# Windowed attention on one core: six buffers, a new slot table, and tokens ordered in column pairs

## The chip, the cores and the metric

The kernel runs on one NeuronCore of one Trainium2 chip. The core has five engines that work at the same time, each on its own queue of instructions: TensorE (PE in the rows, with PEld for its weight loads), VectorE (DVE), ScalarE (ACT), GpSimd (POOL) and SyncE (SP), which here issues all DMAs. They wait for each other on semaphores. The metric is the device time of one execution in microseconds (us), lower is better.

## The reference

Two layers of the same kind act on 64 images of 14 x 14 tokens with 192 channels. Each adds to x an attention of 12 heads of 16 channels over a group norm of x, with a bias of relative positions that is worked out from the query:

```python
x = x + _L0_conv_ref(_gn(x), ...)
x = x + _L1_conv_ref(_gn(x), ...)

qkv = x.reshape(b, hw, dim) @ qkv_w + qkv_b
rel_h = jnp.einsum('bhwc,hkc->bhwk', r_q, Rh)
rel_w = jnp.einsum('bhwc,wkc->bhwk', r_q, Rw)
attn_bias = (rel_h[:, :, :, :, None] + rel_w[:, :, :, None, :]).reshape(b * nH, hw, hw)
attn = jnp.einsum('bqd,bkd->bqk', q, k) * scale + attn_bias
attn = jax.nn.softmax(attn, axis=-1)
out = jnp.einsum('bqk,bkd->bqd', attn, v)
return out @ proj_w + proj_b
```

`rel_h` depends on the image row of the query, so its products take the queries of one image row (14 tokens that lie side by side); `rel_w` depends on the image column (14 tokens that lie 14 apart).

## The kernel before, in words

A unit is one image in one layer, 128 in all. The program is written out as a software pipeline: iteration i has twelve slots, and a job that stands at slot number `at` for its unit is issued in slot `at % 12` of an iteration that is `at // 12` later (negative: earlier) than the unit's own. So jobs of some seven units stand side by side in one iteration, and what an engine does in a slot is fixed by the tables: `JOBS`, `PV_AT`, `MAX_AT`, `EXP_AT` for TensorE, `ACT_LATER` and `DVE_LATER` for the readers of TensorE's results, `POOL_AT` and `SP_AT`. An engine never passes over an instruction that waits: what stands behind it waits too.

TensorE in every slot does one head of the score product for the maxima (`ps_max`, L525) and one head of the score product for the exponentials (`ps_sc`, L538), and then the jobs of that slot:

- xT: transposes the input `xa` (L429), ScalarE copies it to `xT`, VectorE takes statistics (L743), GpSimd the channel's moments (L809, L812);
- g: sums them over a channel group (L435), VectorE copies the result (`gsm`, L791), GpSimd works out the norm (L819 to L830), `xn` (L838), and its float16 halves `xn_hi`, `xn_lo` (L846, L851);
- qk0, qk1, v: projections (L412); queries and keys go as two float16 halves (`qk_hl`, L598 and L734) through DRAM into `q_st` and `k_st`;
- rel0, rel1, rel2: products of q with the position tables for 6, 6 and 2 image rows and as many image columns (L471). Per row or column two row products and two column products, one for each half of the heads, into four groups of 32 PSUM partitions. ScalarE cuts them into a high half (L634 the rows, L643 the columns), VectorE subtracts for the low half (`rel_hl`, L776), and SP brings them into `q_st`;
- mT0, mT1: transposes of the maxima of six heads (L480), ScalarE scales them to `mrow` (L610), and SP brings them into `q_st` as a row of the score product (m0, m1). `ps_sc` of head 0 waits for m0, of head 6 for m1;
- PV: probabilities times v (`ps_o`, L557), ot: transposes of the result (L491), VectorE divides (`rsum` L755, `on` L759), oT: transposes back (L501), y: output projection (L412), ScalarE `yr` (L657), GpSimd adds x to it (`yo`, L862).

The jobs share three PSUM banks. The third entry of a job in `JOBS` is its bank, and `bank_free` makes TensorE wait until the job that had this bank last has been read; the fourth entry says by which semaphore. `ps_max` has two buffers, so the maxima product of a head waits for VectorE's maximum (L722) two heads back.

Input is loaded twice, as `xa` for the transposes and as `xd` for the addition at the end. `q_st`, `k_st` and `v_st` have four buffers each.

## Time and profile before

| | |
|---|---|
| median of 3 runs | 2341.02 us (2326.52 to 2341.86) |
| the profiled execution | 2339.97 us, its span 2338.2 us |
| TensorE busy | 2094.7 us (90%) |
| VectorE busy | 1653.4 us (71%) |
| ScalarE busy | 1621.4 us (69%) |
| GpSimd busy | 714.4 us (31%) |
| DMA moved | 216.34 MB |

The span reaches from the first to the last instruction. Busy time is a share of that span; matmuls overlap, so TensorE's own share says that its queue is seldom empty, not that it works at its peak. In the timelines below a row is one instruction or a run of like ones ("x24"), with its start, the time from the start of the first to the end of the last, and, in brackets, how long the engine was idle before it and what ended that.

### The profile page before, as it was taken

To read this page: it belongs to the slowest core of one execution; us is meant where nothing else is said; L and a number is where in the kernel's file an instruction comes from. 1 tells how busy PE (TensorE), PEld (TensorE's weight loads), DVE (VectorE), ACT (ScalarE), POOL (GpSimd) and SP (SyncE) were. 2 spreads that over 40 slices of the span, in tenths; PEclk is the share of its full clock that TensorE was granted. 3 is DMA by queue.
4 is the path that set the end of the run, shared out by engine and by line. 5 is a ranking of instruction groups with operands and counts; after the bars stand their busy time and mean duration, and the time that the engine had idled before them with its cause. 6 is when DMAs were issued, how large, how long until landed. Compare 5 with 4: busy or idle time off the path is not lost.

```text
span 2338.2 us, 73485 instructions
## 1 busy us (share of the span) xinstructions
PE 2094.7 (90%) x27904; PEld 1595.9 (68%) x27904; DVE 1653.4 (71%) x3923; ACT 1621.4 (69%) x3713; POOL 714.4 (31%) x1796
## 2 busy tenths in 40 slices
...
GB/s 47 84 94 95 104 91 105 91 92 91 103 93 97 90 94 93 101 93 93 91 98 91 94 103 96 88 96 100 91 91 102 94 100 93 94 93 103 91 92 47
DMA packets 170550, 216.34 MB, mean 93 GB/s; under 512 B 29783, under 2 KB 138072, under 8 KB 170202
## 3 DMA queue, kind: packets, MB, share of 16 engines
...
q14 instruction: 122, 1.00, 0.2%
...
## 4 chain that ended last, share of the span: by engine, by line
PE 39%; DMA 33%; SPq 14%; DVE 6%; issue 4%; ACT 3%; POOL 1%; POOLq 0%; ACTq 0%; DVEq 0%
PE ps_m L412 18%; DMA q_st<-mrow 17%; DMA k_dram<-qk_hl 10%; PE ps_sc L538 7%; PE ps_max L525 6%; SPq L375 6%; DMA q_dram<-qk_hl 6%; DVE qk_hl L734 4%; PE ps_o L557 3%; SPq L382 3%; ACT qk_hl L598 2%; SPq L341 2%; SPq L387 2%; PE ps_m L501 2%; DVE rel_hl L776 1%
## 5 line engine op out<-in xcount | busy, mean ns | idle before, releaser
L722 DVE TENSOR_REDUCE mx<-ps_max 98x2 f32<-98x392 f32 x1536 | 819.4, 562 | 232.6 <-PE ps_max L525 215.5
L586 ACT ACTIVATE probs<-ps_sc 98x392 f32<-98x392 f32 x1536 | 714.5, 497 | 232.3 <-PE ps_sc L538 198.2
L525 PE MATMUL ps_max<-k_st,q_st 124*98 124x196 f16 x3072 | 548.9, 261 | 82.4 <-DVE mx L722 82.1
L538 PE MATMUL ps_sc<-q_st,k_st 125*98 125x196 f16 x3072 | 523.3, 252 | 95.6 <-DMA q_st<-mrow 94.1
L776 DVE TENSOR_TENSOR rel_hl<-ps_m,rel_hi 64x504 f16<-64x504 f32 (+1 forms) x768 | 431.4, 562 | 162.0 <-ACT rel_hi L643 152.9
L525 PEld LDWEIGHTS ps_max<-k_st,q_st 124*98 124x98 f16 x3072 | 295.0, 126 | 296.4 <-issue 198.0
L538 PEld LDWEIGHTS ps_sc<-q_st,k_st 125*98 125x98 f16 x3072 | 320.9, 126 | 123.1 <-DMA q_st<-mrow 120.4
L557 PE MATMUL ps_o<-probs,v_st 98*32 98x196 f32 x6144 | 389.6, 340 | 0.5 <-ACT o_sb L578 0.5
L634 ACT ACTIVATE rel_hi<-ps_m,is_lo 64x504 f16<-64x504 f32 (+1 forms) x384 | 223.9, 583 | 189.1 <-PE ps_m L471 185.7
L471 PE MATMUL ps_m<-q_st,rel_st 64*32 64x84 f16 x7168 | 341.6, 266 | 4.8 <-DVE rel_hl L776 4.5
L809 POOL TENSOR_TENSOR msq<-mv 96x2 f32<-96x2 f32 x128 | 24.4, 191 | 1007.1 <-DVE mv L748 1007.1
L643 ACT ACTIVATE rel_hi<-ps_m,is_lo 64x504 f16<-64x504 f32 (+1 forms) x384 | 226.0, 589 | 4.7
L471 PEld LDWEIGHTS ps_m<-q_st,rel_st 64*32 64x32 f16 x7168 | 174.9, 99 | 76.4 <-DVE rel_hl L776 5.1
L557 PEld LDWEIGHTS ps_o<-probs,v_st 98*32 98x32 f32 x6144 | 134.4, 108 | 135.6 <-issue 74.9
L734 DVE TENSOR_TENSOR qk_hl<-ps_m,qk_hl 128x392 f16<-128x392 f32 (+1 forms) x256 | 107.1, 459 | 149.3 <-ACT qk_hl L598 149.3
L412 PE MATMUL ps_m<-xn_hi,w_hi 98*128 98x196 f16 (+1 forms) x768 | 193.5, 252 | 10.5 <-POOL xn_lo L851 10.5
L412 PE MATMUL ps_m<-xn_lo,w_hi 96*128 96x196 f16 x768 | 192.3, 250 | 0.0
L412 PE MATMUL ps_m<-xn_hi,w_lo 96*128 96x196 f16 x768 | 191.7, 250 | 0.0
L819 POOL TENSOR_TENSOR msq<-gsm 96x2 f32<-96x2 f32 x128 | 24.6, 192 | 481.7 <-DVE gsm L791 481.7
L598 ACT CAST qk_hl<-ps_m 128x392 f16<-128x392 f32 (+1 forms) x256 | 103.6, 405 | 86.5 <-PE ps_m L412 83.3
L491 PE MATMUL ps_m<-ident,o_sb 128*98 128x68 f32 x1536 | 151.7, 247 | 0.4 <-ACT o_sb L578 0.4
L862 POOL TENSOR_TENSOR yo<-yr,xd 98x384 f32<-98x384 f32 x128 | 128.0, 1000 | 60.5 <-ACT yr L657 60.5
...
## 6 DMA issues: line engine op xcount, KB each, us to landing
q_st<-q_dram SPq DMA_DIRECT2D x128, 294.0 KB, 3.8
...
q_dram<-qk_hl SPq DMA_DIRECT2D x128, 147.0 KB, 2.6
k_dram<-qk_hl SPq DMA_DIRECT2D x128, 147.0 KB, 2.7
...
```

Of the source, the lines that this page charges most:

```text
L412: last = nc.tensor.matmul(dst, weights(a, c, k), moving(b, c, k), start=n == 0, stop=n == len(terms) - 1)
L471: last = nc.tensor.matmul(to, rel_st[:, lay, axis, w:w + RW], q[:, :, a * SIDE:a * SIDE + SIDE] if axis == 0 else q[:, :, a::SIDE], start= ...
L491: last = nc.tensor.matmul(ps[0:HT, at:at + HG * (HD + 1)], o_sb[p2][:, g, h * HT:h * HT + HT], ident[:, :].rearrange("p (j x) -> p j x", x ...
L525: last = nc.tensor.matmul(ps_max[head % 2][0:HT, h * TOK:h * TOK + TOK], q_st[u.r][0:R_MAX, head, h, :], k_st[u.r][0:R_MAX, head, :], star ...
L538: last = nc.tensor.matmul(ps_sc[head % 2][0:HT, kt * TOK:kt * TOK + TOK], k_st[u.r][0:STACK, head, kt * HT:kt * HT + HT], q_st[u.r][0:STAC ...
L557: last = nc.tensor.matmul(ps_o[32 * j:32 * j + 32, 0:TOK], v_st[u.r][:, kt, head_of(head), :], p[:, kt, :], start=kt == 0, stop=kt == 1)
L586: nc.scalar.activation(probs[head][:, :, :], ps_sc[head % 2][0:HT, 0:2 * TOK].rearrange("p (k t) -> p k t", k=2), ACT.Exp, scale=1.0 / (QS ...
L634: nc.scalar.activation(dst, src, ACT.Identity, scale=is_lo[0:64, 0:1])
L643: nc.scalar.activation(dst, src, ACT.Identity, scale=is_lo[64:128, 0:1])\
L722: nc.vector.reduce_max(mx[u.r % 2][:, head, :], ps_max[head % 2][0:HT, 0:2 * TOK].rearrange("p (q k) -> p q k", q=2), axis=AX.X).then_inc( ...
L734: nc.vector.tensor_tensor(qk_hl[u.r % 2][:, 1, at, :], ps_m[BANK[f"qk{j}"]][:, 0:len(tiles) * TOK].rearrange("p (c t) -> p c t", t=TOK), q ...
L776: last = nc.vector.tensor_tensor(l, src, h, ALU.subtract)
```

## The change

1. **Token order.** Within each pair of image rows the tokens now stand column by column: token (2k + r, b) is at place 28k + 2b + r instead of 14(2k + r) + b. ScalarE puts them so when it copies `xT` out of PSUM, and back when it copies `o_sb`. A column product now reads runs of two elements, 28 apart, where it read single ones, 14 apart; a row product reads every second element where it read 14 side by side. The same holds for where they write in PSUM (for rel0 and rel1; rel2's row products write 84 in a row).
2. **Buffers.** `q_st`, `k_st`, `v_st` have six buffers, `xa` has eight; `xd` and its DMA are gone, and GpSimd adds `xa`.
3. **Slots and banks.** All slot tables and the order of the jobs change; so do the three banks.
4. **Setup.** The one-hot rows of `k_st` are copied from a float16 tile in the new order, 72 copies instead of 48, and two more `v_st` are set.

```diff
+VB = 6
+QB = 6
+XB = 8
...
-        LEAD, TAIL = 1, 6
-        MAX_AT, EXP_AT = 28, 40
...
+        LEAD, TAIL = 2, 7
+        MAX_AT, EXP_AT = 30, 42
+
+        PV_AT = {(0, 0): 45, (0, 1): 46, (1, 0): 50, (1, 1): 52, (2, 0): 55, (2, 1): 55}
+        O_LATER = 2
+
+        JOBS = [(36, "mT0", 0, (s_mrow, 2, 1)),
+                (1, "qk0", 2, (s_qklo, 2, 1)),
...
-        ACT_LATER = {"qk": 0, "mT": 1, "oT": 0, "xT": 0, "rel": 0, "v": 0, "y": 0}
-        DVE_LATER = {"bn": 2, "g": 0, "ot": 0, "oT": 0, "qk": 0, "rel": 0}
-
-        POOL_AT = {"mv": -11, "group": -3, "xn": -1, "xhi": 0, "xlo": 0, "y": 63}
+        ACT_LATER = {"qk": 0, "mT": 0, "oT": 0, "xT": 0, "rel": 0, "v": 0, "y": 1}
+        DVE_LATER = {"bn": 3, "g": 0, "ot": 0, "oT": 3, "qk": 1, "rel": 1}
+
+        POOL_AT = {"mv": -6, "group": -3, "xn": -1, "xhi": 2, "xlo": 5, "y": 82}
         QK_TILES = ((0, 1), (2,))

-        SP_AT = {"m0": 39, "m1": 46, "rel": 22, "qk_out": 3, "q_in": 3, "k_in": 4, "xd": 55, "out": 69, "xa": -12}
+        SP_AT = {"m0": 39, "m1": 41, "rel": 23, "qk_out": 6, "q_in": 7, "k_in": 6, "out": 80, "xa": -15}
...
                                 if axis == 0:
-                                    to = to.rearrange("p (h a b) -> p h a b", h=HH, a=rows)[:, :, i, :]
+                                    to = to.rearrange("p (h k b r) -> p h k r b", h=HH, r=2, b=SIDE)[:, :, i // 2, i % 2, :]
+                                    q = q.rearrange("p h (k b r) -> p h k r b", r=2, b=SIDE)[:, :, a // 2, a % 2, :]
                                 else:
-                                    to = to.rearrange("p (x b) -> p x b", b=rows)[:, :, i]
...
+                                    to = to.rearrange("p (x b r) -> p x b r", b=rows, r=2)[:, :, i, :]
+                                    q = q.rearrange("p h (k b r) -> p (h k) b r", r=2, b=SIDE)[:, :, a, :]
+                                last = nc.tensor.matmul(to, rel_st[:, lay, axis, w:w + RW], q, start=True, stop=True)
...
-            for i in range(UNROLL):
+            dve.wait_ge(s_oh, 1)
+            for i in range(QB):
                 for head in range(HEADS):
-                    nc.vector.tensor_copy(k_st[i][R_REL:STACK, head, :], oh_raw[R_REL:STACK, :])
+                    nc.vector.tensor_copy(k_st[i][R_REL:STACK, head, :], oh_f16[R_REL:STACK, :])
...
-                        nc.gpsimd.tensor_tensor(yo[p2][:, :, :], yr[p2][:, :, :], xd[p2][:, :, :], ALU.add)\
+                        nc.gpsimd.tensor_tensor(yo[p2][:, :, :], yr[p2][:, :, :], xa[u.n % XB][:, :, :], ALU.add)\
```

The slots of an iteration, in which TensorE's jobs stand (numbers modulo twelve; every slot begins with one head of `ps_max` and one of `ps_sc`, and PV stands last in its slot):

| slot | before | of the change |
|---|---|---|
| 0 | y | mT0 |
| 1 | PV | qk0 |
| 2 | | qk1, PV |
| 3 | qk0, qk1, xT, PV | y, xT |
| 4 | | PV |
| 5 | rel0, mT1 | |
| 6 | rel1, PV twice | rel0, mT1 |
| 7 | g | rel1, PV twice |
| 8 | ot, rel2, PV | g |
| 9 | PV | ot, rel2, PV |
| 10 | oT, v | oT, PV |
| 11 | mT0 | v |

The job g of the next unit and ot of an earlier one, as they stand in TensorE's queue behind rel1 and its PV, before. The rows give line, operation, output and inputs, shape, and the semaphores that are waited for; `s_mrow` tells that ScalarE has read the maxima's transposes, `s_rlo` that VectorE has read a rel result:

```order
L557 MATMUL ps_o<-probs,v_st 32x196 x7
L525 MATMUL ps_max<-k_st,q_st 98x196 [waits s_mx]
L525 MATMUL ps_max<-k_st,q_st 98x196
L538 MATMUL ps_sc<-q_st,k_st 98x196 [waits s_p]
L538 MATMUL ps_sc<-q_st,k_st 98x196
L435 MATMUL ps_m<-mv,gmat 96x4 [waits s_mrow,s_mv]
L525 MATMUL ps_max<-k_st,q_st 98x196 [waits s_mx]
L525 MATMUL ps_max<-k_st,q_st 98x196
L538 MATMUL ps_sc<-q_st,k_st 98x196 [waits s_p]
L538 MATMUL ps_sc<-q_st,k_st 98x196
L491 MATMUL ps_m<-ident,o_sb 98x68 [waits s_rlo,s_o]
```

The same place of the change (L433 is g, L488 is ot; `s_g` tells that VectorE has read g's result):

```order
L554 MATMUL ps_o<-probs,v_st 32x196 x7
L522 MATMUL ps_max<-k_st,q_st 98x196 [waits s_mx]
L522 MATMUL ps_max<-k_st,q_st 98x196
L535 MATMUL ps_sc<-q_st,k_st 98x196 [waits s_p]
L535 MATMUL ps_sc<-q_st,k_st 98x196
L433 MATMUL ps_m<-mv,gmat 96x4 [waits s_rlo,s_mv]
L522 MATMUL ps_max<-k_st,q_st 98x196 [waits s_mx]
L522 MATMUL ps_max<-k_st,q_st 98x196
L535 MATMUL ps_sc<-q_st,k_st 98x196 [waits s_p]
L535 MATMUL ps_sc<-q_st,k_st 98x196
L488 MATMUL ps_m<-ident,o_sb 98x68 [waits s_g,s_o]
```

The order of the jobs is the same, but g is now in the bank of rel0 and waits for its reader, and ot is in the bank of g and waits for g's reader; before, g had the bank of mT1 and ot that of rel0.

VectorE's queue at the same place, before (L776 is `rel_hl`, in turn of rel0 and rel1, L791 reads g):

```order
L776 TENSOR_TENSOR rel_hl<-ps_m,rel_hi 64x6x84 [waits s_rhi,s_rel0]
L776 TENSOR_TENSOR rel_hl<-ps_m,rel_hi 64x84x6
L722 TENSOR_REDUCE mx<-ps_max 98x2 [waits s_sm_ps]
L776 TENSOR_TENSOR rel_hl<-ps_m,rel_hi 64x6x84 [waits s_rhi]
L776 TENSOR_TENSOR rel_hl<-ps_m,rel_hi 64x84x6
L722 TENSOR_REDUCE mx<-ps_max 98x2 [waits s_sm_ps]
L791 COPY gsm<-ps_m 96x4 [waits s_gp,s_g_ps]
L722 TENSOR_REDUCE mx<-ps_max 98x2 [waits s_sm_ps]
L755 RECIPROCAL rsum<-ps_m 98x24 [waits s_ot_ps]
```

And of the change:

```order
L725 TENSOR_REDUCE mx<-ps_max 98x2 [waits s_sm_ps]
L779 TENSOR_TENSOR rel_hl<-ps_m,rel_hi 64x6x84 [waits s_rhi,s_rel3]
L779 TENSOR_TENSOR rel_hl<-ps_m,rel_hi 64x42x12
L725 TENSOR_REDUCE mx<-ps_max 98x2 [waits s_sm_ps]
L779 TENSOR_TENSOR rel_hl<-ps_m,rel_hi 64x6x84 [waits s_rhi]
L779 TENSOR_TENSOR rel_hl<-ps_m,rel_hi 64x42x12
L794 COPY gsm<-ps_m 96x4 [waits s_gp,s_g_ps]
L725 TENSOR_REDUCE mx<-ps_max 98x2 [waits s_sm_ps]
L758 RECIPROCAL rsum<-ps_m 98x24 [waits s_ot_ps]
```

The copy of g's result stands directly behind the second subtraction of rel1, where a maximum stood between them; the subtraction of rel0 stands one slot later, behind one more maximum.

GpSimd's queue of the change, over one unit (L864 is the addition that ends a unit, `yo`). Before, `yo` stood ahead of the first L819, behind the moments:

```order
L822 TENSOR_TENSOR msq<-gsm 96x2 [waits s_g]
L825 TENSOR_TENSOR gvar<-gsm,msq 96x2 [waits s_gp]
L828 TENSOR_TENSOR gvar<-gvar,eps 96x2 [waits s_gp]
L831 TENSOR_TENSOR rstd<-gvar,halfpow 96x2 [waits s_gp]
L833 TENSOR_SCALAR nmean<-gsm 96x2
L864 TENSOR_TENSOR yo<-yr,xa 98x384 [waits s_out1,s_yr]
L839 TENSOR_TENSOR anchor<-eps 96x2 [waits s_gp]
L841 TENSOR_SCALAR xn<-xT,nmean,rstd 96x196 x2
L848 TENSOR_TENSOR anchor<-eps 96x2 [waits s_v_ps,s_xn]
L849 CAST xn_hi<-xn 96x392
L854 TENSOR_TENSOR xn_lo<-xn,xn_hi 96x392 [waits s_xhi]
```

The addition has moved between the work on g's result and `xn`, so it stands ahead of what qk0 waits for.

## Rows read from the trace of the kernel before

**Rows 1.** The page's shares: busy us, share of span, instructions.

```profile
PE 2094.7 (90%) x27904; PEld 1595.9 (68%) x27904; DVE 1653.4 (71%) x3923; ACT 1621.4 (69%) x3713; POOL 714.4 (31%) x1796
```

**Rows 2.** One line's view, ot: count, ns min/median/max, first and last start.

```profile
L491 PE MATMUL ps_m<-ident,o_sb x1536: 223/248/302, 115.0 to 2328.5; 128*98 128x68 f32 x192
```

**Rows 3.** Waits: who waited for whom, total us, times, longest.

```profile
PE ps_sc L538 <- DMA q_st<-mrow: 94.1, 105, 2.1
```

**Rows 4.** Timeline of TensorE over one unit: start, length, instruction.

```profile
1005.63 1.10 PE L471 MATMUL ps_m<-q_st,rel_st 64*32 64x84 f16 x24
1006.66 0.25 PE L480 MATMUL ps_m<-ident,mx 98*12 98x98 f32 x1
...
1009.38 0.26 PE L435 MATMUL ps_m<-mv,gmat 96*96 96x4 f32 x2
1010.27 0.37 PE L525 MATMUL ps_max<-k_st,q_st 124*98 124x196 f16 x2 [0.63 <-DVE mx L722]
...
1010.65 1.18 PE L491 MATMUL ps_m<-ident,o_sb 128*98 128x68 f32 x12
1011.76 0.47 PE L471 MATMUL ps_m<-q_st,rel_st 64*32 64x84 f16 x8
1012.17 0.54 PE L557 MATMUL ps_o<-probs,v_st 98*32 98x196 f32 x8
...
1014.55 0.37 PE L538 MATMUL ps_sc<-q_st,k_st 125*98 125x196 f16 x2 [0.60 <-DMA q_st<-mrow]
...
1016.09 0.33 PE L525 MATMUL ps_max<-k_st,q_st 124*98 124x196 f16 x2
...
1022.80 1.10 PE L471 MATMUL ps_m<-q_st,rel_st 64*32 64x84 f16 x24
```

**Rows 5.** Timeline of ScalarE at the same place.

```profile
1006.77 0.68 ACT L634 ACTIVATE rel_hi<-ps_m,is_lo 64x504 f16<-64x504 f32 x1 [0.49 <-PE ps_m L471]
...
1008.56 0.23 ACT L610 ACTIVATE mrow<-ps_m 12x98 f16<-12x98 f32 x1
...
1016.29 0.48 ACT L649 COPY v_st<-ps_m 98x384 f32<-98x384 f32 x1 [0.47 <-PE ps_m L412]
```

**Rows 6.** Timeline of VectorE at the same place.

```profile
1008.24 1.38 DVE L776 TENSOR_TENSOR rel_hl<-ps_m,rel_hi 64x504 f16<-64x504 f32 x2 [1.17 <-ACT rel_hi L643]
1009.65 0.57 DVE L722 TENSOR_REDUCE mx<-ps_max 98x2 f32<-98x392 f32 x1
1010.25 1.37 DVE L776 TENSOR_TENSOR rel_hl<-ps_m,rel_hi 64x504 f16<-64x504 f32 x2
...
1012.14 0.15 DVE L791 COPY gsm<-ps_m 96x4 f32<-96x4 f32 x1
...
1012.68 0.29 DVE L755 RECIPROCAL rsum<-ps_m 98x24 f32<-98x24 f32 x1
1013.01 0.62 DVE L759 TENSOR_TENSOR on<-ps_m,rsum 98x192 f32<-98x192 f32 x2
```

**Rows 7.** Timeline of GpSimd at the same place.

```profile
1007.57 1.00 POOL L862 TENSOR_TENSOR yo<-yr,xd 98x384 f32<-98x384 f32 x1
1012.37 0.19 POOL L819 TENSOR_TENSOR msq<-gsm 96x2 f32<-96x2 f32 x1 [3.79 <-DVE gsm L791]
...
1016.16 0.93 POOL L851 TENSOR_TENSOR xn_lo<-xn,xn_hi 96x392 f16<-96x392 f32 x1
```

**Rows 8.** Windows, L471 alone: stretch, length, PE busy (instructions it touches), PEld, clock.

```profile
1005.63:1005.85 0.22, 0.22 (x16) 0.22 (x18) 1.00 0.00 0
```

**Rows 9.** Timeline of TensorE at the start, at the half clock: rel0 with rel1.

```profile
60.59 2.02 PE L471 MATMUL ps_m<-q_st,rel_st 64*32 64x84 f16 x48 [0.25 <-DVE qk_hl L734]
```

**Rows 10.** TensorE's timeline, one unit later: the wait for m1.

```profile
1032.38 0.50 PE L538 MATMUL ps_sc<-q_st,k_st 125*98 125x196 f16 x2 [1.25 <-DMA q_st<-mrow]
```

**Rows 11.** Windows: PE, PEld, DVE, ACT, POOL busy (instructions), granted clock.

```profile
1032.50:1035.90 3.40, 3.40 (x22) 3.38 (x22) 0.64 (x2) 1.38 (x3) 1.59 (x4) 0.50 0.42 95
1015.30:1018.70 3.40, 3.40 (x45) 3.00 (x43) 2.01 (x4) 2.49 (x8) 1.63 (x4) 1.00 0.41 96
```

More of the change, by code:

```diff
@@ L107, in attention_kernel @@
         anchor = sb("anchor", [CC, 3])
-        q_st = [sb(f"q_st{i}", [128, HEADS, 2, HT], F16) for i in range(4)]
-        k_st = [sb(f"k_st{i}", [128, HEADS, TOK], F16) for i in range(4)]
-        v_st = [sb(f"v_st{i}", [HT, 2, HEADS, PW]) for i in range(4)]
+        q_st = [sb(f"q_st{i}", [128, HEADS, 2, HT], F16) for i in range(QB)]
+        k_st = [sb(f"k_st{i}", [128, HEADS, TOK], F16) for i in range(QB)]
+        v_st = [sb(f"v_st{i}", [HT, 2, HEADS, PW]) for i in range(VB)]
         def pair(name, shape, dt=F32):
             return [sb(f"{name}{i}", shape, dt) for i in range(2)]
-        xa = pair("xa", [HT, 2, C])
+        xa = [sb(f"xa{i}", [HT, 2, C]) for i in range(XB)]
         xT = pair("xT", [CC, 2, TOK])
@@ L143, in attention_kernel @@
         oT_lo = pair("oT_lo", [CC, 2, TOK], F16)
-        xd = pair("xd", [HT, 2, C])
         yr = pair("yr", [HT, 2, C])
@@ L161, in attention_kernel @@
         s_wlo = sem("s_wlo")
+        s_oh = sem("s_oh")
         s_setup = sem("s_setup")
@@ L239, in run @@
                 iteration(lambda lag, i=i: Unit(0, i - lag), min(max(i, 0) // SAMPLES, LAYERS - 1))
-        LEAD, TAIL = 1, 6
-        MAX_AT, EXP_AT = 28, 40
-        PV_AT = {(0, 0): 44, (0, 1): 45, (1, 0): 49, (1, 1): 51, (2, 0): 54, (2, 1): 54}
-        O_LATER = 1
-        JOBS = [(60, "y", 0, (s_yr, 1, 1)),
-                (3, "qk0", 1, (s_qklo, 2, 1)),
-                (3, "qk1", 0, (s_qklo, 2, 2)),
-                (-9, "xT", 2, (s_xT, 1, 1)),
-                (17, "rel0", 0, (s_rlo, 3, 1)),
-                (41, "mT1", 2, (s_mrow, 2, 2)),
-                (18, "rel1", 1, (s_rlo, 3, 2)),
-                (-5, "g", 2, (s_g, 1, 1)),
-                (56, "ot", 0, (s_on, 1, 1)),
-                (20, "rel2", 1, (s_rlo, 3, 3)),
-                (58, "oT", 2, (s_olo, 1, 1)),
-                (10, "v", 0, (s_v, 1, 1)),
-                (35, "mT0", 1, (s_mrow, 2, 1))]
+        LEAD, TAIL = 2, 7
[4 more added lines that the diff above has]
+                (1, "qk0", 2, (s_qklo, 2, 1)),
+                (2, "qk1", 0, (s_qklo, 2, 2)),
+                (63, "y", 2, (s_yr, 1, 1)),
+                (-9, "xT", 1, (s_xT, 1, 1)),
+                (18, "rel0", 0, (s_rlo, 3, 1)),
+                (42, "mT1", 1, (s_mrow, 2, 2)),
+                (19, "rel1", 2, (s_rlo, 3, 2)),
+                (-4, "g", 0, (s_g, 1, 1)),
+                (57, "ot", 0, (s_on, 1, 1)),
+                (21, "rel2", 2, (s_rlo, 3, 3)),
+                (58, "oT", 1, (s_olo, 1, 1)),
+                (11, "v", 0, (s_v, 1, 1))]
         ORDER = [name for _, name, _, _ in JOBS]
@@ L357, in iteration @@
                                 p, r0 = 64 * axis + 32 * half, R_REL + RW * axis
-                                sp.dma_start(q_st[u.r][r0:r0 + rows, half * HH:half * HH + HH, :, :],
+                                sp.dma_start(q_st[u.n % QB][r0:r0 + rows, half * HH:half * HH + HH, :, :],
                                              rel_hl[u.r % 2][p:p + rows, :, :]).then_inc(s_rel[u.r], 16)
@@ L374, in iteration @@
                         for part in range(2):
-                            sp.dma_start(k_st[u.r][2 * HD * part:2 * HD * part + 2 * HD, :, :],
+                            sp.dma_start(k_st[u.n % QB][2 * HD * part:2 * HD * part + 2 * HD, :, :],
                                          k_dram[u.r].rearrange("l d h c t -> d l (h c t)"))\
                               .then_inc(s_kst[u.r], 16)
-                    u = due(unit, s, SP_AT["xd"])
-                    if u:
-                        src, at = (x_in, u.n) if not layer_of(u, layer) else (x1, u.n - SAMPLES)
-                        wait(sp, s_y, u.n - 1)
-                        sp.dma_start(xd[u.r % 2][:, :, :], tokens(src[bass.ds(at, 1)])).then_inc(s_xd[u.r], 16)
                     u = due(unit, s, SP_AT["out"])
@@ L462, in job @@
                             for half in range(2):
-                                q = q_st[u.r][0:R_REL, half * HH:half * HH + HH, :, :]\
+                                q = q_st[u.n % QB][0:R_REL, half * HH:half * HH + HH, :, :]\
                                     .rearrange("p h q t -> p h (q t)")
@@ L647, in iteration @@
                         act.wait_ge(s_v_ps, u.n + 1)
-                        wait(act, s_o_ps, (u.n - 3) * GROUPS)
-                        nc.scalar.copy(v_st[u.r][:, :, :, 0:HD],
+                        wait(act, s_o_ps, (u.n - VB + 1) * GROUPS)
+                        nc.scalar.copy(v_st[u.n % VB][:, :, :, 0:HD],
                                        ps_m[BANK["v"]][0:HT, 0:2 * C]
```

44 lines of the change are left out of this document (22 added, 22 removed).

## The prediction

> **What bounds the kernel now.** I read four views in this order. The page's shares say that TensorE is busy 90% of the span; VectorE's 1653.4 us are 12.9 us for each of 128 units, ScalarE's 1621.4 us are 12.7 [rows 1]. The first and the last start of job ot, which runs once in each unit, give the pace: (2328.5 - 115.0) / 127 = 17.43 us per unit [rows 2]. What lies outside is 2338.2 - 2213.5 = 124.7 us. TensorE's timeline shows one unit from rel0 at 1005.63 to the next at 1022.80, 17.17 us [rows 4]. In it TensorE waits twice: from the end of g (9.38 + 0.10) to 10.27, which is 0.79 us, for VectorE's maximum, and before `ps_sc` of head 6 for the DMA of the maxima m1 (the row's 0.60 us, 0.77 us by starts, since two pipelined products hide some). The second wait varies: 94.1 us over 105 times, up to 2.1 [rows 3]. Without either a unit is 17.17 - 0.79 - 0.77 = 15.61 us of TensorE's own work. So TensorE's queue is the bound, with two waits in it, and the timelines of the others [rows 5 to 7] show why the first is there: rel0 starts on TensorE at 5.63, ScalarE at 6.77, VectorE at 8.24, and VectorE has two subtractions of 1.4 us to do with maxima between them.
>
> **Part 1, the column products.** rel0 has 24 products and lasts from 1005.63 to 1006.66, rel2 has 8 and lasts from 1011.76 to 1012.17 [rows 4]: 0.62 us for 16 more, 0.155 us per image row with its column, and 1.03 - 6 x 0.155 = 0.10 around them. In the first 0.22 us 16 of the 24 products have begun [rows 8]; the remaining 8 take 0.8. The row products run ahead in their own PSUM partitions, and the column products set the pace at 0.155 per pair. At the half clock 48 products take 2.02 us where 24 take 1.10 at the full clock [rows 9, 4], no longer per product, so it is access to memory and not the array that costs. With runs of two there are half as many places to go to. Bounds: 0.155 (nothing gained) and 0.04 (8 row products in 0.22 us are 0.03 per product; a pair at most this); I take the half, 0.077, since the price followed the places. Then rel0 and rel1 take 6 x 0.077 + 0.10 = 0.56, rel2 0.25: TensorE's work falls by 0.47 + 0.47 + 0.16 = 1.10 us, to 14.5 us per unit.
>
> The Trainium skill, "SBUF — State Buffer", section Specifications (TRN2), says that SBUF has lines of 16 bytes and wants at least two hits on each for full bandwidth; by it runs of two float16 go at the full rate, rel0 takes 0.34 instead of 0.56, and the sum below falls by about 0.3 us a unit. The rows cannot decide between that and the half.
>
> **Part 2, buffers.** `xd` goes with one DMA a unit, and the extra buffers remove no wait that the rows show. m1 is issued right after its maxima, six slots before its reader, where it was issued in the reader's slot behind k_in, xd and out. Its wait of 0.77 us goes. SP's queue gets a wait for a landing (k_in right behind qk_out) and one for `yo`, with q_in, out, xa, rel and m0 behind them; their readers stand five slots and more later, except m0's, which is in the sixth slot after it. I cost all this at nothing, since those slots cover it; if m0 were late, it would cost what m1 costs now, up to 0.77.
>
> **Part 3, the slots.** What matters is the chain from rel0 to ot. Count from rel0's first product. Before: ScalarE +1.14, VectorE +2.61 to +3.99, second subtraction +4.62 to +5.99, g's copy +6.51 to +6.66, ot at +5.02 [rows 4, 5, 6]; ot did not have to wait for g's copy, it had the bank of rel0. In the change:
> - rel0 ends at +0.56, the transpose mT1 behind it +0.29 later (0.25 and 0.04 to hand over) at +0.85. ScalarE now scales mT1 first (0.23, done +1.10), then does the two halves of rel0 at 0.68 each, to +2.48; VectorE starts at +2.58 and ends at +3.96. So the faster rel0 buys nothing here: the mT1 in front of it takes its place.
> - TensorE's g waits for that: +4.00, where its queue is ready at 0.56 + 0.09 + 0.43 + 0.56 + 0.81 (two PV) + 0.38 = +2.83. A wait of 1.17.
> - VectorE: maximum, 0.60 as now from 9.65 to 10.25, second subtraction +4.57 to +5.95, g's copy to +6.12. TensorE's ot waits for it: **+6.17**. Ready at 4.09 + 0.38 = +4.47: a wait of 1.70.
> - From ot to the next rel0 stands the same work as before, in another order: 1010.65 to 1022.80 is 12.15, less 0.77 of m1 and 0.16 of rel2: 11.22. Three small waits are new in it. oT (one slot behind ot, was two): ot takes 1.11, VectorE starts 0.17 later and needs 0.95 (12.68 to 13.63), so oT can start 2.28 after ot; TensorE is there after ot, rel2, a PV of 0.47 and a head pair of 0.38, 2.21: 0.07. mT0 now has v's bank: ScalarE's copy of v starts 0.20 after v's end (1016.09 to 1016.29), takes 0.48, 0.05 to hand over, and one head pair of 0.34 covers part: 0.39. qk0 needs `xn_lo`: GpSimd takes 12.37 to 17.09 from g's copy, 4.72 us [rows 7], and `yo` is moved into this stretch, 1.00 more, so qk0 can start at 6.12 + 0.08 + 5.72 + 0.05 = +11.97; by the like pieces of the timeline TensorE is there at +11.9: 0.07.
>
> **Sum: 6.17 + 11.22 + 0.53 = 17.92 us per unit**, of which TensorE waits 3.4, against 1.56 in the unit shown (14.5 + 3.4 agrees). The costs end in ot's wait: what is late next is GpSimd's `xn_lo`, and with it qk0.
>
> **Part 4, the clock.** After the two waits of this unit TensorE's granted clock stayed full; where it had waited 1.25 us for m1 one unit later [rows 10], the clock stood at 0.50, 1.2 GHz instead of 2.4, in the 3.40 us that followed, with 22 instructions against 45 in an equal stretch at full clock [rows 11]. That is 1.7 us lost. In the change TensorE waits 1.17 and then 1.70 us in every unit with 0.5 us of work between. I expect the lower level behind it in most units: 8 in 10, at 1.5 us each (part of a stretch may lie in the wait), is +1.2, less 0.1 of small waits it covers. **Per unit 19.0 us.**
>
> **Part 5, setup.** 24 more copies of 196 columns: at most a maximum's 0.57 us each [rows 6], 14 us, at least nothing if the float16 source makes all 72 faster. The source is half as wide; I take 5.
>
> **Total.** 1.8 us around the span, 124.7 + 5 outside the pace, 127 x 19.0 = 2413: **2545 us**, 205 above the profiled execution of 2339.97, which lies 1 us below the median 2341.02.
>
> **Rivals.**
> - *The same chain, full clock.* 131.5 + 127 x 17.92 = 2407. For it: before, waits of 0.8 did not lower the clock. Against: 1.25 did.
> - *The chain is shorter.* If VectorE or ScalarE get through sooner, so that ot starts near +5.7, and the small waits stay, a unit is 17.4 and the time 2341: no change.
> - *Row products pay.* They now read and write every second element. Should each place in PSUM cost as a column product does now, the row pair goes at 0.155, rel0 stays 1.03: chain +0.47, rel2 +0.16, so +0.6 a unit, 2621. The Trainium skill, "PSUM — Partial Sum Buffer", section Specifications (TRN2), says that lines are 8 bytes and that any access that is not contiguous slows matmuls significantly, which is this; no row shows such an access alone.
> - *Faster, the other side.* If my chain is wrong in its main link and ot does not wait behind VectorE (its wait under about 0.9 decides, at full clock, since then gains of 1.10 + 0.77 win), a unit comes to 15.3, with VectorE's 12.9 below it: 131.5 + 1943 = 2075. Against it stand the queue order and the durations of [rows 6], none of which the change shortens.
>
> **Chances.** Chain with low clock 0.47, chain at full clock 0.22, row products 0.11, shorter chain 0.07, faster 0.13. The range takes the first three: 2395 to 2640. Above 1% is what a measurement of this kernel tells from no change. Faster by over 1%: 0.13. Within 1%: 0.06. Slower: 0.81.
>
> **What would show it.** Right: TensorE's largest waits are g for `rel_hl` (about 1 us a unit) and ot for `gsm` (about 1.5), both absent now; the waits for m1 are gone; rel0's 24 products take 0.56; the mean granted clock falls from 0.98 to about 0.9, in stretches right behind ot's start. GpSimd's `xn_lo` appears as what ends a wait of qk0. Wrong: TensorE's ot starts less than 5.6 us behind rel0, or the wait for `gsm` is under 0.5 us a unit; then the pace is TensorE's own work, near 15. Rows at 0.155 a pair would show as rel0 at 1.0 us.

## The result and the profile after

| | before | after |
|---|---|---|
| median | 2337.26 us (4 runs, 2326.52 to 2341.86) | 2832.02 us (4 runs, 2829.27 to 2835.07) |
| ratio | | 1.2125, 95% interval 1.2076 to 1.2174 |
| span of the profiled execution | 2338.2 us | 2827.7 us |
| mean granted clock of TensorE | 0.98 | 0.798 |
| one unit, from starts of ot | 17.43 us | 21.25 us |

The change makes the kernel 21% slower. The direction was forecast; the size was not: 2545 us, with 2640 as the upper end. Executions more than 1.5% above the fastest of their kernel count as slow, and ratios and medians here go by the others.

The shares on the page of after, and the granted clock in 40 slices of the span:

```profile
PE 2418.8 (86%) x27904; PEld 1856.1 (66%) x27904; DVE 1688.4 (60%) x3950; ACT 1609.7 (57%) x3713; POOL 708.7 (25%) x1796
...
PEclk9777877877887787788778778877877887787788
```

TensorE is busy for longer than before [rows 1] with the same number of instructions, though its column products are cheaper. The digits of the clock say why: 7 and 8 all through.

The line of ot, in the view of one line, and the waits of TensorE by line, in us, times and the longest:

```profile
L488 PE MATMUL ps_m<-ident,o_sb x1536: 248/273/434, 119.0 to 2817.9; 128*98 128x68 f32 x192
```

```profile
PE ps_m L488 <- DVE gsm L794: 185.9, 123, 1.5
PE ps_m L433 <- DVE rel_hl L779: 142.7, 126, 2.1
...
PE ps_m L477 <- ACT v_st L649: 5.5, 25, 0.3
```

The pace is (2817.9 - 119.0) / 127 = 21.25 us, 3.82 above [rows 2]; 127 times that is 485 of the 489.5 us between the spans. The first two rows are the two waits that were forecast, one of each in nearly every unit, and the waits for m1 [rows 3] have no row any more.

TensorE's timeline over one unit of after (L471 rel, L477 mT, L433 g, L488 ot, L554 PV):

```profile
1014.29 0.62 PE L471 MATMUL ps_m<-q_st,rel_st 64*32 64x84 f16 x24
1014.85 0.25 PE L477 MATMUL ps_m<-ident,mx 98*12 98x98 f32 x1
...
1018.39 0.30 PE L433 MATMUL ps_m<-mv,gmat 96*96 96x4 f32 x2 [1.12 <-DVE rel_hl L779]
...
1020.58 2.23 PE L488 MATMUL ps_m<-ident,o_sb 128*98 128x68 f32 x12 [1.51 <-DVE gsm L794]
1022.75 0.46 PE L471 MATMUL ps_m<-q_st,rel_st 64*32 64x84 f16 x8
1023.14 0.88 PE L554 MATMUL ps_o<-probs,v_st 98*32 98x196 f32 x8
...
1029.70 0.24 PE L477 MATMUL ps_m<-ident,mx 98*12 98x98 f32 x1
...
1036.00 0.63 PE L471 MATMUL ps_m<-q_st,rel_st 64*32 64x84 f16 x24
```

The same stretch in windows (stretch, length, busy time of PE, PEld, DVE, ACT, POOL with instructions, then the granted clock, the share that the DMA engines are busy, and GB/s):

```profile
1014.00:1018.00 4.00, 3.27 (x78) 2.13 (x75) 3.27 (x10) 3.88 (x9) 0.38 (x2) 1.00 0.13 27
1018.00:1022.00 4.00, 2.10 (x15) 1.96 (x16) 2.80 (x6) 1.78 (x4) 1.25 (x4) 0.68 0.49 119
1022.00:1026.00 4.00, 4.00 (x37) 2.37 (x36) 2.06 (x6) 1.76 (x4) 3.84 (x9) 0.50 0.53 130
1026.00:1030.00 4.00, 3.99 (x28) 3.47 (x25) 1.13 (x2) 1.43 (x5) 0.06 (x1) 0.54 0.39 101
1030.00:1034.00 4.00, 4.00 (x51) 3.53 (x49) 3.01 (x6) 2.49 (x7) 0.00 (x0) 1.00 0.00 1
```

The clock falls from 2.4 to 1.2 GHz within the stretch that holds the second wait (in halves of a microsecond it is 0.94 in 1019.0:1019.5 and 0.50 from then on, so here it falls some 0.4 us into that wait), and stays there through ot, rel2, the probability products, oT and all of v. ot's twelve products take 2.17 us to the start of rel2, where they took 1.11 before [rows 4]. It is full again by 1030, some 9 us behind ot's start. That is the rule and not this unit alone: the mean clock of 0.798 means 2 x 0.202 x 2827.7 = 1142 us at half speed, and the trace has 126 stretches at the lower level, 9.1 us long on average, one for nearly each of the 128 units. The kernel before has 20, of 5.1 us on average.

ScalarE and VectorE behind rel0 in after:

```profile
1015.13 0.24 ACT L609 ACTIVATE mrow<-ps_m 12x98 f16<-12x98 f32 x1
1015.40 0.68 ACT L634 ACTIVATE rel_hi<-ps_m,is_lo 64x504 f16<-64x504 f32 x1
```

```profile
1016.87 1.37 DVE L779 TENSOR_TENSOR rel_hl<-ps_m,rel_hi 64x504 f16<-64x504 f32 x2 [0.68 <-ACT rel_hi L643]
1018.27 0.57 DVE L725 TENSOR_REDUCE mx<-ps_max 98x2 f32<-98x392 f32 x1
1018.87 1.37 DVE L779 TENSOR_TENSOR rel_hl<-ps_m,rel_hi 64x504 f16<-64x504 f32 x2
1020.28 0.16 DVE L794 COPY gsm<-ps_m 96x4 f32<-96x4 f32 x1
```

Counted from rel0's start at 1014.29, ScalarE's first half stands at +1.11, the subtractions at +2.58 and +4.58, g at +4.10, ot at +6.29.

### The profile page after: what moved, and what is told of

Read it like the earlier page. It is cut to its first block, busy times and chain, and to the rows that moved or that the text cites. A ratio compares the mean times of both kernels' runs of the same rounds, so it can differ in the third digit from the quotient of the medians.

```text
span 2827.7 us, 73380 instructions
## 1 busy us (share of the span) xinstructions
PE 2418.8 (86%) x27904; PEld 1856.1 (66%) x27904; DVE 1688.4 (60%) x3950; ACT 1609.7 (57%) x3713; POOL 708.7 (25%) x1796
## 4 chain that ended last, share of the span: by engine, by line
PE 64%; DVE 16%; ACT 11%; issue 7%; POOL 1%; ACTq 0%; DMA 0%; DVEq 0%; SPq 0%; POOLq 0%
PE ps_m L410 21%; DVE rel_hl L779 12%; PE ps_o L554 11%; PE ps_max L522 10%; PE ps_m L488 8%; PE ps_sc L535 8%; ACT rel_hi L643 3%; ACT rel_hi L634 3%; PE ps_m L498 3%; DVE mx L725 2%; ACT probs L585 2%; PE ps_m L427 2%; ACT o_sb L575 1%; PE ps_m L471 1%; PE ps_m L477 1%
## 5 line engine op out<-in xcount | busy, mean ns | idle before, releaser
L522 PE MATMUL ps_max<-k_st,q_st 124*98 124x196 f16 x3072 | 619.7, 289 | 0.4 <-DVE mx L725 0.4
L535 PE MATMUL ps_sc<-q_st,k_st 125*98 125x196 f16 x3072 | 589.1, 278 | 0.7 <-ACT probs L585 0.7
L554 PE MATMUL ps_o<-probs,v_st 98*32 98x196 f32 x6144 | 475.1, 403 | 1.7 <-ACT o_sb L575 0.9
L535 PEld LDWEIGHTS ps_sc<-q_st,k_st 125*98 125x98 f16 x3072 | 385.5, 146 | 3.5 <-ACT probs L585 2.6
L488 PE MATMUL ps_m<-ident,o_sb 128*98 128x68 f32 x1536 | 218.0, 309 | 191.0 <-DVE gsm L794 185.9
L488 PEld LDWEIGHTS ps_m<-ident,o_sb 128*98 128x98 f32 x1536 | 197.8, 219 | 213.9 <-issue 207.4
L554 PEld LDWEIGHTS ps_o<-probs,v_st 98*32 98x32 f32 x6144 | 145.5, 119 | 132.5 <-issue 87.1
L471 PE MATMUL ps_m<-q_st,rel_st 64*32 64x84 f16 x7168 | 221.3, 266 | 2.9 <-DVE rel_hl L779 2.7
L410 PE MATMUL ps_m<-w_hi,xn_hi 98*98 98x192 f16 (+1 forms) x512 | 187.6, 366 | 0.3 <-DVE gsm L794 0.3
L410 PE MATMUL ps_m<-w_lo,xn_hi 96*98 96x192 f16 x512 | 187.6, 366 | 0.0
L410 PE MATMUL ps_m<-w_hi,xn_lo 96*98 96x192 f16 x512 | 187.6, 366 | 0.0
```

The costliest lines, as they stand in the source:

```text
L410: last = nc.tensor.matmul(dst, weights(a, c, k), moving(b, c, k), start=n == 0, stop=n == len(terms) - 1)
L471: last = nc.tensor.matmul(to, rel_st[:, lay, axis, w:w + RW], q, start=True, stop=True)
L488: last = nc.tensor.matmul(ps[0:HT, at:at + HG * (HD + 1)], o_sb[p2][:, g, h * HT:h * HT + HT], ident[:, :].rearrange("p (j x) -> p j x", x ...
L522: last = nc.tensor.matmul(ps_max[head % 2][0:HT, h * TOK:h * TOK + TOK], q_st[u.n % QB][0:R_MAX, head, h, :], k_st[u.n % QB][0:R_MAX, head ...
L535: last = nc.tensor.matmul(ps_sc[head % 2][0:HT, kt * TOK:kt * TOK + TOK], k_st[u.n % QB][0:STACK, head, kt * HT:kt * HT + HT], q_st[u.n % ...
L554: last = nc.tensor.matmul(ps_o[32 * j:32 * j + 32, 0:TOK], v_st[u.n % VB][:, kt, head_of(head), :], p[:, kt, :], start=kt == 0, stop=kt == 1)
```

## The experiments

**1. How much is chain, how much is clock.** My theory was that the chain of waits gives the pace at full clock and the rest is the clock. So I left every wait's end where it is and gave TensorE something to do until then: unread score products, into the buffer that its next maxima product overwrites.

```diff
+            def filler(unit, s, n):     # n products of the next head, read by nobody
+                ...
+                    for i in range(n):
+                        nc.tensor.matmul(ps_max[head % 2][0:HT, i % 2 * TOK:i % 2 * TOK + TOK], ...)
...
                     for name in ORDER:
+                        if due(unit, s, AT[name]) and name in ("g", "ot"):
+                            filler(unit, s, {"g": 12, "ot": 16}[name])
                         job(name, unit, s, layer)
```

> The changed kernel with products that nobody reads in its two waits: 12 ahead of g and 16 ahead of ot, copies of the next head's maxima product into the free ps_max buffer, about 1.0 and 1.35 us at full clock, less than the waits of 1.1 and 1.5 us that they stand in. The chain of waits is not touched. Theory (the waits lengthen the unit to about 18 us, and the rest, 3.3 us a unit, is TensorE's clock, which is low behind them): the mean granted clock goes back to 0.97 or more, a unit takes 17.9 to 18.2, the time is 2400 to 2450 us. Rival (the 3.3 us come from something else, contention or more waits further on): the clock does not matter, and the time stays at 2800 or more.

Measured: 2395.38 us (ratio to before 1.0225, 1.0172 to 1.0278), clock 0.998, with 3516 more matmuls than after. Its timeline and its line of ot:

```profile
1011.48 0.63 PE L471 MATMUL ps_m<-q_st,rel_st 64*32 64x84 f16 x24
...
1014.30 1.17 PE L517 MATMUL ps_max<-k_st,q_st 124*98 124x196 f16 x12
...
1016.10 1.53 PE L517 MATMUL ps_max<-k_st,q_st 124*98 124x196 f16 x16
1017.77 0.45 PE L488 MATMUL ps_m<-ident,o_sb 128*98 128x68 f32 x3
```

```profile
L488 PE MATMUL ps_m<-ident,o_sb x1536: 225/248/312, 117.1 to 2384.1; 128*98 128x68 f32 x192
```

ot starts at +6.29, as in after, yet the unit is (2384.1 - 117.1) / 127 = 17.85 us against 21.25. So of after's 3.82 us, 0.42 is the chain and 3.40 is the clock: 53 and 432 us of the whole. (The 17.43 of before holds a clock loss of its own: at a mean clock of 0.978 it spends 0.8 us of a unit at half speed, worth 0.4 at most. With full clock on both sides the chain costs up to 0.8.) Work that nobody reads makes the kernel 437 us faster than waiting.

**2. Which wait, and what stands behind it.** Two kernels: the filler ahead of ot alone, and no filler in the waits but twelve unread products behind ot, ahead of rel2.

```diff
+                        if due(unit, s, AT[name]) and name in {"ot": 16}:       # e9_filler_ot
+                        if due(unit, s, AT[name]) and name in {"rel2": 12}:     # e9b_filler_behind
```

> The changed kernel with the unread products ahead of ot alone (16, about 1.35 us); the wait of 1.1 us ahead of g stays empty. With both filled the clock was 0.998 and a unit 17.85 us. Theory A (either wait alone is like those of the kernel before, which lowered the clock now and then): clock 0.93 to 0.99, 18.0 to 18.7 us a unit, 2415 to 2510 us. Theory B (one wait of 1.1 us in each unit is enough to keep the clock low): 2650 or more.

> The changed kernel with 12 unread maxima products (1.0 us at full clock, 2.0 at half) not in a wait but behind ot, ahead of rel2, where TensorE has work. Both long waits stay. If only the waits decide how long the clock stays low, a unit is 1 to 2 us longer than 21.25: 2950 to 3080 us. If the work that stands behind the waits (transposes, products with 32 weights) is what lets the clock stay low for 6.8 to 10.2 us, the added work pays for itself: at or below 2830.

Measured: 2423.17 us for the first (1.0365, 1.0284 to 1.0446), clock 0.975, with g's wait untouched:

```profile
PE ps_m L433 <- DVE rel_hl L791: 142.3, 126, 2.5
```

A wait of 1.12 us in each unit alone leaves the clock nearly full (23 stretches at the lower level in the whole trace, against 126). With the second one, of 1.51, which begins 0.7 us behind the first, it falls in nearly every unit. No run keeps the second wait and fills the first, so whether 1.51 us would do it alone is not shown; the single waits of 1.6 and 1.7 us of experiment 3 do. The second kernel (one execution): 2723.4 us, clock 0.907. TensorE around ot:

```profile
1005.43 1.67 PE L488 MATMUL ps_m<-ident,o_sb 128*98 128x68 f32 x12 [1.51 <-DVE gsm L806]
1006.89 2.17 PE L517 MATMUL ps_max<-k_st,q_st 124*98 124x196 f16 x12
1008.99 0.46 PE L471 MATMUL ps_m<-q_st,rel_st 64*32 64x84 f16 x8
1009.38 0.55 PE L566 MATMUL ps_o<-probs,v_st 98*32 98x196 f32 x8
```

```profile
1009.00:1009.50 0.50, 0.50 (x13) 0.24 (x16) 0.00 (x0) 0.00 (x0) 0.42 (x3) 0.54 0.79 228
```

Both waits are there (184.1 and 143.7 us in all), and the clock still falls (in this unit 0.6 us behind ot's start: 0.55 in 1006.0:1006.5), but PV at 1009.38 takes 0.55 where after's takes 0.88: the level is full again 4 us behind ot's start instead of 9. Over the whole trace there are 126 stretches at the lower level as in after, but of 4.0 us on average instead of 9.1. Per unit it costs (2712.0 - 116.4) / 127 = 20.44, less 17.85, less some 1.0 for the twelve added products: 1.6 instead of 3.4. So adding work behind the wait takes 109 us off, and with the waits unchanged, other work behind them changed how long the clock stays low. The one instance in before did not tell this. There, behind the wait of 1.25 us [rows 10], stood this:

```profile
1032.68 0.86 PE L501 MATMUL ps_m<-ident,on 98*96 98x98 f32 x4
1033.33 0.36 PE L412 MATMUL ps_m<-w_hi,xn_hi 98*98 98x192 f16 x1
...
1035.90 0.25 PE L480 MATMUL ps_m<-ident,mx 98*12 98x98 f32 x1
```

v's twelve products came at once, and mT0 behind them is at full speed. In after 6.3 us of ot, rel2, PV and oT come first, and again it is behind v that the clock is full. (That wait was also another one, 1.25 us alone, so these two instances differ in more than the work behind.) Which property of ot, rel2 and PV keeps it low was not told apart.

**3. One number of the table.** If g's place in the banks makes ot late, moving g back should undo it in after and do it in before.

```diff
-                (-4, "g", 0, (s_g, 1, 1)),      # after: e2_g_bank1
+                (-4, "g", 1, (s_g, 1, 1)),
-                (-5, "g", 2, (s_g, 1, 1)),      # before: e3_before_g_bank0
+                (-5, "g", 0, (s_g, 1, 1)),
```

> The changed kernel with g in bank 1 (where the transposes of the maxima stand) instead of bank 0: g no longer waits for rel0's reader, and ot waits for rel0's reader instead of g's. Theory (the banks of g and ot make the two long waits, and these lower the clock): the waits of g for rel_hl and of ot for gsm go; ot starts about 4.0 us behind rel0 instead of 6.3, but rel2 then waits for rel1's reader, oT for on, qk0 for xn_lo, each under 1 us, so a unit takes 17.2 to 18.0 at a clock above 0.95: 2320 to 2450 us. Rival (the slot table as a whole is at fault, whatever the bank): 2750 or more.

> The kernel before with one number changed: g in bank 0, so that g waits for rel0's reader and ot for g's. Theory: ot starts 6.6 to 6.7 us behind rel0 instead of 5.0, with a wait of about 1.6 us for gsm that was not there, and the clock falls behind it as in the changed kernel: 19 us a unit from the wait and 2 to 3 more from the clock, 2700 to 2900 us. Rival (buffers, token order or GpSimd's order make the loss): within 2% of before, 2300 to 2390.

Measured on before: 2820.47 us (1.2039, 1.1978 to 1.2101), clock 0.824. One number gives nearly the whole loss of the change. Here the long wait stands nearly alone: the wait for m1 is gone, and g and the maximum wait 0.24 and 0.21 us on average.

```profile
PE ps_m L491 <- DVE gsm L791: 199.0, 123, 1.6
```

```profile
1018.03 2.24 PE L491 MATMUL ps_m<-ident,o_sb 128*98 128x68 f32 x12 [1.62 <-DVE gsm L791]
```

Measured on after: 2642.17 us (1.1278, 1.1217 to 1.134), clock 0.824. g no longer waits, and ot starts at +5.18 instead of +6.29, but waits again:

```profile
1006.51 0.63 PE L471 MATMUL ps_m<-q_st,rel_st 64*32 64x84 f16 x24
...
1011.69 1.67 PE L488 MATMUL ps_m<-ident,o_sb 128*98 128x68 f32 x12 [1.71 <-ACT o_sb L575]
```

```profile
1010.22 0.68 ACT L643 ACTIVATE rel_hi<-ps_m,is_lo 64x504 f16<-64x504 f32 x1
1010.92 0.50 ACT L585 ACTIVATE probs<-ps_sc 98x392 f32<-98x392 f32 x1
1011.32 0.32 ACT L575 COPY o_sb<-ps_o 128x196 f32<-128x196 f32 x1
```

The copy that ot reads stands on ScalarE behind both halves of rel1 and an exponential, and is late by itself; in after it ends at +5.12 (1019.09 and 0.32 us) and was hidden behind the wait for `gsm`. I had not seen this one. So ot is held by two things in after, and setting right only one gives back 190 us.

**4. The token order alone, and after without it.**

> The kernel before with the new token order alone: no other slot, bank or buffer. Theory: rel0 and rel1 take 0.56 instead of 1.03 us each, rel2 about 0.3 instead of 0.41; the chain behind rel0 starts 0.47 sooner and TensorE's work is 1.1 us less, so a unit gets 0.6 to 1.1 us shorter unless the wait for m1, which hangs on the DMA queue, grows by as much: 2200 to 2270 us. Rival (the product's time is hidden behind the waits for VectorE and for m1): 2330 to 2350.

> The changed kernel with the old token order (column products read single elements again); slots, banks and buffers stay as changed. Theory (what sets the unit is the chain rel0 - ScalarE - VectorE - g - rel1's reader - gsm - ot, and rel0's length is its first member): rel0 goes back to 1.03 us, ot starts 0.47 later, rel2 takes 0.1 to 0.16 more, so a unit is 0.5 to 0.6 us longer: 2880 to 2920 us. TensorE's waits grow by nothing, since it has 0.47 more work of its own in the same stretch. Rival (the new order costs elsewhere, in PSUM reads of ScalarE or in the clock, and was part of the loss): at or below the changed kernel, 2750 to 2835.

Before with the new order (part 1 of the change and its setup): 2400.96 us (1.0255, 1.0205 to 1.0305), clock 0.927. TensorE's work falls and the kernel gets slower. Its waits, and under them the first of these rows in the kernel before, whose second is [rows 3]:

```profile
PE ps_max L526 <- DVE mx L729: 133.6, 130, 1.4
PE ps_sc L539 <- DMA q_st<-mrow: 130.9, 105, 2.6
```

```profile
PE ps_max L525 <- DVE mx L722: 82.1, 130, 1.6
```

TensorE reaches both places sooner, waits longer (88 us in all), and the clock is lower: by its mean some 250 us more at half speed, worth up to 125. Together they outweigh the 140 us of work saved. After with the old order is at 2872.75 us (1.2288, 1.2191 to 1.2385), so in after the new order is worth 41 us. That is less than its 1.1 us a unit (140 us); 56 of the missing 99 are in g's wait, which is 86.2 us in all there and 142.7 with the new order. Most of the rest is the clock, 0.819 there and 0.798 with the new order: some 100 us more at half speed, worth up to 50.

**5. Reading or writing.** What made a column product cost 0.155 us? In before, I let the column products keep their reads of single elements and write 84 side by side; and the reverse. Either way the results then stand, or come from, the wrong places, so the bias of columns is not the reference's.

```diff
-                                    to = to.rearrange("p (x b) -> p x b", b=rows)[:, :, i]     # e10_write_runs
+                                    to = to[:, i * HH * SIDE:(i + 1) * HH * SIDE]
...
-                                    q[:, :, a * SIDE:a * SIDE + SIDE] if axis == 0 else q[:, :, a::SIDE],     # e11_read_runs
+                                    q[:, :, a * SIDE:a * SIDE + SIDE],
```

> The kernel before in which a column product still reads single elements 14 apart, but writes its 84 results side by side in PSUM (they then stand in the wrong places, so the bias of columns is not the reference's; all instructions and shapes of the other engines are the same). It parts the two places where a column product has steps. If the reading sets its 0.155 us a pair, rel0 stays at 1.03 us and the time at 2320 to 2350. If the writing sets it, rel0 falls to about 0.35 us and the time by some 20 to 60 us or not at all (the waits for VectorE and m1 take it up, as the new order alone showed).

> The counterpart: a column product reads 14 elements side by side (those of an image row, so the bias of columns is not the reference's) and writes single results 6 or 2 apart as before. If reading sets the price, rel0 falls to about 0.35 us; if writing does, it stays at 1.03. If both have a part, both runs are in between.

rel0 with what follows it, first the kernel that writes in runs, then the one that reads in runs:

```profile
1003.34 1.09 PE L471 MATMUL ps_m<-q_st,rel_st 64*32 64x84 f16 x24
1004.36 0.25 PE L480 MATMUL ps_m<-ident,mx 98*12 98x98 f32 x1
```

```profile
1000.53 0.62 PE L471 MATMUL ps_m<-q_st,rel_st 64*32 64x84 f16 x24
1001.08 0.25 PE L480 MATMUL ps_m<-ident,mx 98*12 98x98 f32 x1
```

1.02 us against 0.55. Reading single elements was the whole of that difference; beside such reads the strided writes cost nothing that shows (1.02 without them, 1.03 with them). Runs of fourteen give 0.55 and the change's runs of two 0.56, so two elements already reach what fourteen do. In both of these the column products still write in strides, and no kernel reads and writes them in runs, so whether the writes have a part in the 0.55 is not shown. What the traces do show is that it goes with the clock. At the start, where the clock is at half, rel0 and rel1 in after take

```profile
62.97 1.86 PE L471 MATMUL ps_m<-q_st,rel_st 64*32 64x84 f16 x48 [0.25 <-DVE qk_hl L737]
```

against 0.56 + 0.63 = 1.19 at full clock, while before took 2.02 at half [rows 9] and 1.03 + 1.10 = 2.13 at full. So the new order saves 0.9 us of these two at full clock and 0.16 at half. The kernels took 2368.25 and 2435.44 us (one execution each, clock 0.976 and 0.914): the one with the cheaper rel0 is the slower one, as in experiment 4, with 133.7 us waited for the maximum and 125.8 for the maxima's DMA.

**6. Take the wait away first, then the work.** If waits turn saved work into a loss, the order pays once the wait for m1 is gone: in before, m1 is issued four slots sooner, and k_in two later.

```diff
-        SP_AT = {"m0": 39, "m1": 46, "rel": 22, "qk_out": 3, "q_in": 3, "k_in": 4, ...
+        SP_AT = {"m0": 39, "m1": 42, "rel": 22, "qk_out": 3, "q_in": 3, "k_in": 6, ...
```

> The kernel before with two numbers of SP's table changed: m1 issued at 42 instead of 46, and k_in two slots later, so that m1 stands ahead of k_in. Theory: its landing is some 2 us ahead of its reader, the wait of 94 us in all for it goes and with it the stretches at the lower clock: 17.43 becomes 16.4 to 16.7 us a unit, 2210 to 2250 us, clock 0.99. Rival (the wait only moves to k_in's reader or to VectorE): 2310 or more.

> The same with the new token order, otherwise the kernel before. The order alone made it slower, with 131 us of waits for m1 and 134 for VectorE's maxima and a clock of 0.927. Theory (a shorter rel0 pays when no long wait stands beside it): ot starts 4.55 behind rel0 and the next rel0 11.2 behind ot, 15.8 us a unit, if the clock holds 2120 to 2150; the wait of 1.04 for the maxima stays in each unit and may lower the clock in some, up to 2250. Rival (the new order has a cost of its own of 60 us or more): slower than the run with m1 alone.

The two numbers alone: 2200.24 us (0.9411, 0.9354 to 0.9468), clock 0.995. With the new order too: 2158.6 us (0.9233, 0.9157 to 0.931), from the two faster of four executions, 2153.25 and 2164.0; the other two took 2193.86 and 2204.3, and the median of all four is the 2178.93 that the last expectation below starts from. The clock of the profiled one is 0.977, an undisturbed unit 15.73 us, where 15.8 was worked out. The order that cost 60 us in before brings 42 here (21 by the median of all four). That is less than its 1.1 us a unit (140) because the one wait left has grown from 0.61 to 1.04, 82.3 to 134.4 us in all, and the clock has fallen from 0.995 to 0.977, some 75 us more at half speed:

```profile
1007.63 0.37 PE L526 MATMUL ps_max<-k_st,q_st 124*98 124x196 f16 x2 [1.04 <-DVE mx L729]
```

Then I moved the subtraction of rel behind a maximum (`DVE_LATER` of rel 0 to 1, rel2 at 21), which takes this wait away.

> The kernel before with the new token order, m1 early, and two numbers more: VectorE subtracts rel one slot later (as in the change), and rel2 stands one slot later in TensorE's queue. The banks stay those of before, so ot does not wait for gsm. Theory: the maxima no longer stand behind the wait for ScalarE's rel_hi, so the last wait of 1.04 us a unit goes, against about 0.1 for rel_hl ahead of ot and 0.3 for on ahead of oT: 15.73 becomes 15.0 to 15.4 us a unit at a clock of 0.99, 2040 to 2090 us. Rival (the wait only moves to ot, rel2 or oT, as it did in the change): 2150 or more.

2214.8 us (0.9468, 0.9423 to 0.9513), clock 0.974. The wait for the maximum is gone, and ot has got one, as the rival had it. The input's transposes now wait for `xa` too, 50.3 us in 88 places, where the kernel before this one had 7.4:

```profile
PE ps_m L492 <- ACT o_sb L579: 113.7, 118, 1.2
PE ps_m L431 <- DMA xa<-x: 26.8, 46, 1.9
```

Last, without that move, the wait of 1.04 us was left and ten unread products (into `ps_sc`, which the next score product overwrites) put into it, behind g.

```diff
                         job(name, unit, s, layer)
+                        if name == "g" and due(unit, s, AT[name]):
+                            filler(unit, s, 10)
```

> The kernel before with the new token order and m1 issued early (as e7_before_order_m1, 2178.93 us, mean clock 0.977, 15.99 us a unit on average where an undisturbed unit takes 15.73), and ten unread score products into ps_sc behind g, that is in the stretch in which TensorE otherwise waits 1.04 us a unit for VectorE's maximum. Theory: of e7's pace, 15.99 - 15.73 = 0.26 us a unit is what the lower clock costs; work in the wait holds the clock at the full level, the wait is replaced by work of about the same length, and the time is 2178.93 - 127 x 0.26 = about 2146 (2125 to 2165), clock above 0.99. Rival: the clock of e7 falls behind other waits than this one, or ten products last longer than the wait: then the clock stays near 0.98 or the pace near 16, and the time is 2170 to 2210.

```profile
1011.07 1.02 PE L521 MATMUL ps_sc<-q_st,k_st 125*98 125x196 f16 x10
1012.25 0.37 PE L536 MATMUL ps_max<-k_st,q_st 124*98 124x196 f16 x2 [0.15 <-DVE mx L741]
```

```profile
L492 PE MATMUL ps_m<-ident,o_sb x1536: 222/249/372, 107.9 to 2105.3; 128*98 128x68 f32 x192
```

2116.76 us (0.9017, 0.8968 to 0.9067), clock 0.995: the best of all, 220 us below the 2337.26 of before, with nothing left out. The mean pace is now that of the undisturbed unit, (2105.3 - 107.9) / 127 = 15.73 us. It is 8 us below the range that I gave, because I worked out the clock's loss, 0.26 us a unit, from the profiled execution of the kernel without the filler, which was its fastest (span 2151.5 us), and took it off the median of 2178.93. Off that execution's own 2153.25 it gives 2120.

The clock of these kernels (without the two of experiment 5) beside TensorE's waits in a unit, each the total of its row divided by its times:

| kernel | waits in a unit, us | clock |
|---|---|---|
| after, filler in both waits | 0.32 | 0.998 |
| before, order, m1, filler behind g | 0.19 | 0.995 |
| before, m1 | 0.63 | 0.995 |
| before | 0.63, and 0.90 for m1 (up to 2.1) | 0.98 |
| before, order, m1 | 1.03 | 0.977 |
| after, filler ahead of ot | 1.13, 0.32 | 0.975 |
| before, order, m1, rel later | 0.96, and 0.57 for `xa` | 0.974 |
| before, order | 1.03, and 1.25 for m1 (up to 2.6) | 0.927 |
| after, filler behind ot | 1.14 and 1.50, 0.32 | 0.907 |
| before, g in bank 0 | 1.62, 0.24, 0.21 | 0.824 |
| after, g in bank 1 | 1.69 | 0.824 |
| after, old order | 0.68 and 1.51 | 0.819 |
| after | 1.13 and 1.51 | 0.798 |

## Why the prediction was wrong in size

**The failed step is Part 4, the clock.** It said 1.5 us lost in 8 of 10 units, 1.2 less 0.1 for covered small waits. Measured: 3.40 us a unit (experiment 1). With that value in the sum, 131.5 + 127 x (17.92 + 3.40) = 2839, against 2832.02. Three things went wrong. The length of the low stretch was taken from one instance in before, 3.4 us, as if it were the chip's own, where the 20 in the trace of before are 5.1 on average; behind ot it is 9.1. It hangs on the work behind the waits (experiment 2: with the same waits 4.0 us on average, and a loss of 1.6 against 3.4 a unit); that v at once made the instance in before short fits this, but was not run alone. The clock fell in nearly every unit, and not in 8 of 10. And the range had no end for this term: its upper bound of 2640 came from the row products, while the clock got a single value, though no row showed how long it stays low behind ot. The whole stretch from ot to v at half speed, about 9 us with 4.5 lost, was the bound from the other side; it gives some 2980. The mean clock, forecast at about 0.9, is 0.798.

**Part 1 held in size and not in reason.** rel0 takes 0.56, as forecast, and rel2 0.26 at full clock against 0.25. But it wasn't half the price because half the places are read: runs of fourteen give no more (experiment 5). The rule of the Trainium skill, "SBUF — State Buffer", section Specifications (TRN2), that two hits on a line are enough for the full rate, is what the runs agree with (0.56 in runs of two, 0.55 in runs of fourteen). The 0.34 that I worked out from it is not reached: something other than the length of the read runs then holds rel0 at 0.55, and it goes with the clock.

**Part 2 held.** The waits for m1 are gone. SP's new waits are there in its own queue (252.4 us for the landing ahead of k_in, 236.2 for `yo`), but none reaches TensorE; m0's reader does not wait either.

**Part 3 held.** ScalarE +1.11 (forecast +1.10), subtractions +2.58 and +4.58 (+2.58, +4.57), g +4.10 with a wait of 1.12 (+4.00, 1.17), ot +6.29 with 1.51 (+6.17, 1.70). At full clock the unit is 17.85 against 17.92. Of the small waits the one of mT0 is 0.32 (40.3 us over 126 in the kernel with the filler, forecast 0.39) and nearly vanishes in after (5.5 us over 25), where the slow work covers it. Those of oT and qk0, 0.07 each, don't appear, so the sign that `xn_lo` would end a wait of qk0 failed. What Part 3 missed is `o_sb`, which would have held ot to +5.18 anyway (experiment 3).

**Part 5.** Outside the pace lie 2827.7 - 2698.9 = 128.8 us, 4 above before, against the forecast 5 in setup.

**The rivals.** The chain at full clock, 2407, is what the filler shows (2395.38), but the change itself isn't that case. Row products at 0.155 are out: rel0 would have stayed at 1.03. The rule of the Trainium skill, "PSUM — Partial Sum Buffer", section Specifications (TRN2), that any access which is not contiguous slows matmuls significantly, is not borne out where the runs can tell. The row products with their stride of two cost nothing that shows (rel0 0.56, against 0.55 where they stay contiguous), and no more do the strided column writes beside single reads (1.03 against 1.02); for column writes beside reads in runs it is open. In rel2 of the change the row products write every second place as well, not 84 in a row as the description of the change has it. The faster rival, ot not behind VectorE, fell with the chain.
